# Twelve split pairs, VectorE's layer-1 lows from hi copies in PSUM, and layer 2's split tiles behind the plain tiles of the next slot

## What is computed

```python
for idx, (W, b) in enumerate([(w0, b0), (w1, b1), (w2, b2)]):
    z = relu(einsum('bhd,bkd,hks->bsd', x0, xk, W) + b)
    # layers 0 and 1: first 64 rows are the next xk, the other 64 go to direct;
    # layer 2: all 128 rows go to direct
logit = sum over d of concatenate(direct)           # 256 values a row
h = relu([logit, dense] @ W_top1 + b_top1)          # 272 -> 512
h = relu(h @ W_top2 + b_top2)                       # 512 -> 256
y = h @ W_top3                                      # 256 -> 1
```

## Time and profile before

| | us |
|---|---|
| median of three runs | 2544.88 |
| lowest, highest | 2543.24, 2546.89 |
| the profiled execution, its own time | 2545.02 |
| its span, first to last instruction | 2543.1 |
| TensorE busy | 2432.8 |
| VectorE busy | 2268.7 |
| GpSimd busy | 1557.9 |
| ScalarE busy | 1175.5 |

### The profile page before, as it was taken

How to read it: one execution, slowest core, us unless ns; L and a number is a source line. 1 busy time by engine, 2 the same in 40 slices (tenths; PEclk the granted TensorE clock), 3 DMA queues, 4 the chain that set the end, 5 groups by cost and what they waited for, 6 DMA issues and landing times.

```text
span 2543.1 us, 25999 instructions
## 1 busy us (share of the span) xinstructions
PE 2432.8 (96%) x7712; PEld 1423.5 (56%) x7712; DVE 2268.7 (89%) x1356; ACT 1175.5 (46%) x1414; POOL 1557.9 (61%) x1029
## 2 busy tenths in 40 slices
PE   0599999999999999999999999999999999999999
PEld 0265555556555555555555565555556555555553
DVE  0599999999999999999999999999999999999960
ACT  0244444445454444545444444444444444445442
POOL 6476667667666766766676666667666766743240
PEclk9899999999999999999999999999999999999999
DMA  2986777777677777867777776787777677766610
GB/s 69 246 211 180 199 207 202 180 217 214 176 198 205 207 178 215 209 182 197 209 206 177 217 206 190 190 211 210 178 207 205 200 184 213 207 182 194 195 30 0
DMA packets 262712, 477.02 MB, mean 188 GB/s; under 512 B 19500, under 2 KB 37788, under 8 KB 262614
## 3 DMA queue, kind: packets, MB, share of 16 engines
q1 hardware_dynamic: 141766, 271.07, 38.9%
q10 hardware_dynamic: 100480, 200.29, 28.5%
q0 software_dynamic: 20448, 5.45, 1.4%
HBM read 468.99 MB, written 7.74 MB: 187 GB/s over the span
## 4 chain that ended last, share of the span: by engine, by line
PE 73%; POOL 10%; DVE 6%; issue 4%; DMA 4%; ACT 2%; SPq 0%; POOLq 0%; DVEq 0%; ACTq 0%
PE z L693 37%; PE z L716 33%; POOL emb L352 5%; DVE prod L418 4%; POOL pair_lo L211 4%; DMA emb<-in_tbl,idx 3%; PE xk L775 1%; PE z L775 1%; DMA x_pairs<-x_transposed 1%; ACT pair_hi L532 1%; POOL half_parts L207 1%; DVE pair_lo L211 1%; PE turned L674 1%; DVE logit L448 1%; ACT xk L542 0%
## 5 line engine op out<-in xcount | busy, mean ns | idle before, releaser
L418 DVE TENSOR_TENSOR prod<-x_pairs,xk 128x2048 f32<-128x2048 f32 x640 | 1436.4, 2284 | 75.2 <-PE z L716 46.9
L693 PE MATMUL z<-prod,w_plain 128*128 128x512 f32 (+2 forms) x2944 | 1383.1, 594 | 40.5 <-DVE prod L418 40.5
L532 ACT CAST pair_hi<-prod 128x1024 fp32r<-128x1024 f32 x703 | 735.4, 1046 | 1085.2 <-PE z L716 793.6
L211 POOL TENSOR_TENSOR pair_lo<-prod,pair_hi 128x1024 fp32r<-128x1024 f32 x320 | 764.1, 2388 | 638.3 <-ACT pair_hi L532 621.7
L693 PEld LDWEIGHTS z<-prod,w_plain 128*128 128x128 f32 (+2 forms) x2944 | 555.4, 189 | 474.1 <-issue 394.9
L352 POOL DMA_INDIRECT emb<-in_tbl,idx x624 | 701.3, 1124 | 184.0 <-issue 173.7
L716 PE MATMUL z<-pair_hi,w_lo 128*128 128x512 f32 (+1 forms) x1408 | 786.6, 559 | 2.3 <-DVE pair_lo L211 1.7
L716 PE MATMUL z<-pair_hi,w_hi 128*128 128x512 f32 (+1 forms) x1408 | 555.7, 395 | 0.0
L716 PE MATMUL z<-pair_lo,w_hi 128*128 128x512 f32 (+1 forms) x1408 | 555.1, 394 | 0.0
L211 DVE TENSOR_TENSOR pair_lo<-prod,pair_hi 128x1024 fp32r<-128x1024 f32 (+1 forms) x384 | 468.5, 1220 | 48.7 <-ACT pair_hi L532 48.7
L716 PEld LDWEIGHTS z<-pair_hi,w_lo 128*128 128x128 f32 (+1 forms) x1408 | 265.2, 188 | 297.2 <-POOL pair_lo L211 135.8
(11 more groups left out here) (50 smaller groups left out, 566.5 us busy)
## 6 DMA issues: line engine op xcount, KB each, us to landing
x_pairs<-x_transposed SPq DMA_DIRECT2D x64, 2432.0 KB, 16.9
x_pairs<-x_transposed ACTq DMA_DIRECT2D x64, 2432.0 KB, 19.3
x_diag<-x_transposed SPq DMA_DIRECT2D x128, 546.0 KB
x_diag<-x_transposed ACTq DMA_DIRECT2D x64, 546.0 KB
x_pairs<-x_transposed SPq DMA_DIRECT2D x64, 256.0 KB, 20.4
emb<-in_tbl,idx POOLq DMA_INDIRECT x624, 6.3
x_diag<-x_transposed SPq DMA_DIRECT2D x128, 78.0 KB
x_transposed<-stage SPq DMA_DIRECT2D x32, 156.0 KB
```

The lines of the kernel that those rows point to most:

```text
L211: engine.tensor_tensor(pair_lo[0:rows, pair % PAIR_RING], held[0:rows, at:at + 2, :], pair_hi[0:rows, pair % PAIR_RING].bitcast(F32), ALU. ...
L418: nc.vector.tensor_tensor(prod[0:rows, pos % RING, 0:n, :], a, xk.unsqueeze(1).broadcast_to([rows, n, N]), ALU.mult).then_inc(prod_ready, 1)
L532: nc.scalar.copy(pair_hi[0:rows, pair % PAIR_RING], held[:, at:at + 2, :]).then_inc(hi_ready, 1)
L693: ins = nc.tensor.matmul(z[n][:], w, held[0:rows, i, :], start=(k == 0 and i == plain[0]), stop=(k == last_slot and not here and i == plai ...
```

## The change

- **Splits.** Layer 0 splits a second pair (tiles 2 and 3), so there are 12 pairs a chunk. Each split names the engine of its low: layer 1's third pair goes to GpSimd, all others of layers 0 and 1 stay on VectorE.
- **Rings.** The hi and low parts have six tiles (three pairs), with fixed places.
- **Copies in PSUM.** For layer-1 lows of VectorE, ScalarE rounds the products a second time, into `hi_copy` (two PSUM banks, shared with `turned`) or, for the half tile, into the new PSUM bank `direct01`; VectorE subtracts that copy. A second pair copy waits for the low before it. `direct01` is in PSUM, xk0 shares the bank of xk2; so ScalarE waits for layer 0's last product before it writes xk2.
- **Order on VectorE.** A slot's lows always follow the next slot's product; the exception for slot 1 of layer 1 is gone.
- **Order on TensorE.** Layer 2's split tiles follow the plain tiles of the next slot, which frees each slot later. Layer 0 waits for both its slots, does the three last tiles, then the two split pairs, and frees both slots at the end. The transposes move behind layer 0.
- **GpSimd.** Layer 1's low comes first in a chunk, then 9 or 10 gathers, then layer 2's lows. 20 fields of the second group are ahead at the start instead of 30; the indices are loaded after layer 2's lows of chunk 1, the gathers no longer wait for the earlier ones in each chunk, and fields 30 to 38 are gathered in chunk 1.
- **Sums.** logit01 and logit2 hold 512 rows; SP stores a window of 128 rows per group to DRAM, and `load_top` loads the first 1536 rows and the rest back (four more loads).
- **Stage.** `fill_stage` moves behind the hand-on of xk1 and direct_0 in chunk 1, and ScalarE waits for its own copies there.

```diff
-SPLITS = {0: [(0, 0, 2)],
-          1: [(0, 0, 2), (1, 0, 2), (2, 0, 2), (2, 3, 1), (3, 0, 2), (4, 0, 2)],
-          2: [(0, 0, 2), (1, 0, 2), (2, 0, 2), (2, 3, 1), (3, 0, 2), (4, 0, 2)]}
-EARLY = {1: 4, 2: 4}
+SPLITS = {0: [(0, 0, 2, V), (0, 2, 2, V)],
+          1: [(0, 0, 2, V), (1, 0, 2, V), (2, 0, 2, G), (2, 3, 1, V), (3, 0, 2, V), (4, 0, 2, V)],
+          2: [(0, 0, 2, G), (1, 0, 2, G), (2, 0, 2, G), (2, 3, 1, G), (3, 0, 2, G), (4, 0, 2, G)]}
+EARLY = {1: 5, 2: 4}
+BEHIND = {1: False, 2: True}
-GATHERS_AHEAD = 30
-GATHERS_AT = [range(30, F), range(0, 10), range(10, 20), range(20, 30)]
-PAIR_RING = 2
+GATHERS_AHEAD = 20
+GATHERS_AT = [range(20, 30), range(30, F), range(0, 10), range(10, 20)]
+PARTS = 6
...
             def group(bt, fields_at):
...
+                    done = lows_of(1, chunk, 0, split, pos)
+                    if c == 2 and len(fields_at[c]):
+                        start_group(bt + 2, False)
+                    gather(fields_at[c])
...
+                    lows_of(2, chunk, done, split, pos)
+                    if c == 1 and len(fields_at[2]):
+                        pool.wait_ge(gathered, 16 * (bt + 2) * F)
+                        pool.sem_inc(waits_held, 1)
+                        load_indices(bt + 2)
...
             def group(bt, last):
                 for c in range(CHUNKS):
+                    if c == 0:
+                        sp.wait_ge(summed01, bt * CHUNKS + 1)
+                        store_window(0, bt)
+                    if c == 1:
+                        sp.wait_ge(summed2, bt * CHUNKS + 2)
+                        store_window(1, bt)
                     if c == 2 and not last:
                         store_group(bt + 1)
...
+            def products(n, copies, xk, slot, pos, late, split, chunk):
+                first_tile, rows, tiles = (FIRST_TILE, P, TX) if n else (L0_FIRST, R0, T0)
+                for k, first in enumerate(first_tile):
+                    product(slot + k, pos + k, copies[0:rows, first:min(first + QUAD, tiles), :],
+                            xk[0:rows])
+                    split = subtract(late, split)
+                    late = splits_of(n, pos, k, chunk)
+                return late, split
...
+                        act.wait_ge(slot_free, RING + used_by[place + m - 1] + 1)
+                        nc.scalar.copy(hi_parts[0:rows, place:place + m, :], held[:, at:at + m, :]
                                        ).then_inc(hi_ready, 1)
+                    if n and who == V:
+                        copies = [s for s in SPLITS[n][0:i] if s[3] == V]
+                        if m == 1:
+                            nc.scalar.copy(direct01[0:HALF].bitcast(F32R), held[0:HALF, at, :]
+                                           ).then_inc(hi_copied, 1)
+                        else:
+                            if any(s[2] == m for s in copies):
+                                last = max(j for j, s in enumerate(copies) if s[2] == m)
+                                act.wait_ge(lo_ready[V],
+                                            len(SPLITS[0]) + chunk * LOWS_C[V] + last + 1)
+                            nc.scalar.copy(hi_copy[:, 0:m, :].bitcast(F32R), held[:, at:at + m, :]
+                                           ).then_inc(hi_copied, 1)
...
                     if not (last and c == CHUNKS - 1):
+                        round_splits(0, slice(0, None), slot, pos, used_by, chunk)
+                        act.wait_ge(prod_ready, slot + SL0)
                     hand_on(1, xk2, b1_sb, slot)
...
-                    if c == 1 and not last:
-                        fill_stage(bt + 1)
...
                         hand_on(0, xk1, b0_sb, slot)
-                        act.wait_ge(summed01, chunk + 1)
+                        act.wait_ge(summed01, chunk + 2)
                         direct_0()
+                        if c == 1 and not last:
+                            fill_stage(bt + 1)
+                            act.wait_ge(stage_ready, 2 * (bt + 2))
...
+                    for i in plain:
+                        plain_part(n, t, i, held, k == 0 and i == plain[0], False)
+                    if not BEHIND[n]:
+                        split_parts(n, k, lows)
+                    elif k > 0:
+                        split_parts(n, k - 1, lows)
+                if BEHIND[n]:
+                    split_parts(n, last_slot, lows)
+            def layer0(slot, pos, lows):
+                pe.wait_ge(prod_ready, slot + SL0)
+                held = prod[:, (pos + SL0 - 1) % RING]
+                t = L0_FIRST[SL0 - 1]
+                for i in range(T0 - t):
+                    plain_part(0, t, i, held, i == 0, False)
...
+                for i, (s, place) in enumerate(zip(SPLITS[0], PLACES[0])):
+                    ins = split_part(0, 0, s, place, lows, False, i == len(SPLITS[0]) - 1)
+                    lows[s[3]] = lows[s[3]] + 1
+                ins.then_inc(slot_free, SL0)
```

More of the change, by code:

```diff
@@ L78 @@
 NB = 512
-assert CB < NB < B and len(SPLITS[0]) == 1
+assert CB < NB < B and all(k == 0 for k, _, _, _ in SPLITS[0])
 def top_order():
@@ L357, in group @@
             def group(bt, fields_at):
[L358 to L359 removed]
                 for c in range(CHUNKS):
                     chunk = bt * CHUNKS + c
[L363 to L365 removed]
+                    split, pos = len(SPLITS[0]) + chunk * SPLITS_C, SL0 + c * SLC
@@ new lines, in splits_of @@
+            def splits_of(n, pos, slot, chunk):
+                copies, here = lows(1, V) if n == 2 else 0, []
+                for s, place in zip(SPLITS[n], PLACES[n]):
+                    copy = chunk * COPIES_C + copies if n else None
+                    copies += s[3] == V
+                    if s[0] == slot:
+                        here.append((n, pos, copy, place, *s))
+                return here
+            def products(n, copies, xk, slot, pos, late, split, chunk):
[6 more added lines that the diff above has]
+                return late, split
@@ L456, in sum2 @@
                                         z[2][:].rearrange("p (d b) -> p b d", b=CB),
                                         AXIS.X, ALU.add).then_inc(summed2, 1)
-            def layer(n, copies, xk, slot, pos):
-                return [(n, k, copies, xk, slot + k, pos + k) for k in range(SLX if n else SL0)]
-            products(layer(0, x0_diag, xk0, 0, 0), 0, 0, 0)
+            dve.wait_ge(xk0_ready, 1)
+            late, split = products(0, x0_diag, xk0, 0, 0, [], 0, 0)
+            subtract(late, split)
@@ L490, in group @@
                         if k == 1:
-                            sum01(chunk)
-                    pair = pair_after + PAIRS[2]
+                            sum01(bt, c)
+                        split = subtract(late, split)
+                        late = splits_of(2, pos, k, chunk)
+                    subtract(late, split)
             with dve.Fori(0, GROUPS - 1) as bt:
@@ L677, in transpose_group, with plain_part @@
                         ins.then_inc(turned_ready, 1)
-            def layer(n, slot, pos, split, pair):
-                whole, hi, lo, splits = w_plain[n], w_hi[n], w_lo[n], SPLITS[n]
-                first_tile = FIRST_TILE if n else L0_FIRST
-                last_slot = len(first_tile) - 1
-                for k, t in enumerate(first_tile):
+            def plain_part(n, t, i, held, first, last):
+                rows = P if n else R0_LAST if t + i == T0 - 1 else R0
+                w = w_plain[n][0:rows, PLAIN_TILES[n].index(t + i), :]
+                return nc.tensor.matmul(z[n][:], w, held[0:rows, i, :], start=first, stop=last)
```

310 lines of the change are left out of this document (167 added, 143 removed).

## The result

The changed kernel takes 2575.95 us (four runs, 2574.12 to 2577.07) against 2544.27 before: a ratio of 1.0122, 95% interval [1.0105, 1.014]. The forecast was 2500. The profiled execution took 2574.12 us, 29 more than the one of before.

What follows compares the result with a forecast made beforehand. TensorE's work plus three late layer-2 lows was taken to bound the loop. Ordinary periods -40, transposing ones -4.7 and start +0.6 total -44 us: 2545.0 becomes 2501, 2500 at the median; range 2484 to 2534.

Steps and rivals of the forecast that it cites:

- Ordinary periods: Main-loop chunks without transposes: from 36.69 to 35.8 us, -0.85 x 47 = -40 us.
- The +0.10: Per chunk, us added for what is late next: layer 2's last pair and VectorE's stalled layer-1 product.
- the change does not free layer 2: Rival: layer 2's last pair's low stays late by some 0.5 us a chunk; +25 us, 2525; chance 0.12.
- Prices of VectorE: Layer-1 lows with a PSUM operand stay at 1.22 us; the reduce over direct01 falls from 1.06 to 0.69.
- The slower rival: Layer 1's four pairs: dearer PSUM lows make VectorE the bound; 2600 us, far bound 2780; chance 0.08.
- PSUM copies: Layer 1: lows reading one PSUM operand no longer stretch gathers, which took 1.58 us instead of 0.94.
- Gathers and transposes: Chunk 1: last gather starts near T + 16, transposes wanted at T + 20.6; transposing period 37.5 us.
- gathers late: Rival, before the transposes: gathers land 2 us later than taken, 6.6 us each; +30 us, 2530; chance 0.12.
- the 0.7 taken: Us of wait before the transposes, between no wait with 3.5 us to land and 2.0 with 6.6.
- x_diag: Loads behind SP's stage stores: out at +18, needed by +30; cost zero, margin 2 to 3 us.
- the rival's 2 us: Rival: x_diag loads late once a group, from SP's queue order; 2 us x 15, 2530; chance 0.05.
- Start: Kernel start: xk0's copy goes in front of the first pairs' load, +0.6 us.

Runs made afterwards that it cites:

- e5_stage_early: Changed kernel with three of nine gathers before layer 1's low and the stage copy behind layer 2's first two hi parts; 2500.45 us, ratio 0.9808.
- f3_stage_three: e5_stage_early with the stage copy behind three hi parts of layer 2 instead of two; 2519.57 us, ratio 0.9905.
- e7_sbuf_lows: Changed kernel without ScalarE's PSUM copies, VectorE's layer-1 lows reading the hi parts in SBUF; one run, 2663.44 us.
- e1_early3: Changed kernel with three of chunk 1's nine gathers issued before GpSimd's layer-1 low; 2631.23 us, ratio 1.0329.
- e2_fill3: Changed kernel with three extra plain matmuls, result unused, in front of the transposes; 2553.24 us, ratio 1.0023.
- e3_early1: Changed kernel with one of chunk 1's nine gathers issued before GpSimd's layer-1 low; 2654.71 us, ratio 1.0412.

## Why the prediction was wrong, point by point

- **Ordinary periods: right.** 35.8 us was forecast and measured, and the 41 us they give match the forecast's 40. The weight loads' wait for GpSimd fell from 135.8 us to 3.1. The +0.10 was right by luck. It stood for a late last pair and late products, and neither is there: the end of a chunk with the last pair takes 4.53 us on average in the changed kernel, 4.52 being its undisturbed length. TensorE's own slots, from start to start, add up to 35.8, where the prediction's rounded ones gave 35.7 (its step of 0.85 for 36.69 - 35.8 = 0.89 is another slip of that size). The late last pair came in e5_stage_early, where no stall hands GpSimd any slack: there it costs 0.2 us a chunk on average. The rival "the change does not free layer 2" had this mechanism, at 0.4. The marks of the periods are VectorE's, so a single period can be shorter than TensorE's need (35.38 in f3_stage_three, behind a stall).
- **Prices of VectorE: right.** 1.21 for the PSUM low, -0.375 for the reduce; VectorE works 34.7 us in the ordinary period (34.9 forecast), ScalarE 22.8 (23.6), GpSimd 26.95 (27.0). The slower rival, through dearer PSUM lows, is out, and with it the figures of the Trainium skill (VectorE: DVE Perf Modes, The TRN2 errata), by which a PSUM source has the larger fixed cost. These rows show 1212 against 1213 ns and contradict it for these two forms of 1024 columns.
- **PSUM copies: mis-sized.** The prediction counted stretched gathers only. e7_sbuf_lows puts the copies at 1.7 us a period (one run). It changed no number of the forecast, since the kernel keeps the copies.
- **Gathers and transposes: the step that failed.** The text took the last gather at T + 16, a stretch of 0.8 us, and 3.5 us to land, although the trace of before showed 6.6 for today's last gather. It explained those 6.6 by the pair loads beside it. (In that group TensorE went on 5.96 us after the gather's start, on the same count; but in 11 of 15 groups of that trace TensorE waited for the gathers, up to 0.96 us, and they landed after 6.1 to 6.9 us.) The runs show T + 17.0, a stretch of 1.9 and 6.9 us, with no DMA busy at the end. The rival "gathers late" had the place and the mechanism, and its 2 us over the 0.7 taken come to 2.7, near the 3.2 measured. It was given 0.12 and should have been the forecast: the row with 6.6 was there, and the reason against it was an assumption about the pair loads.
- **The term that was missing: the clock.** The rival's 2530 left out what a stall of TensorE does behind it. It is 2.7 us a group, 40 us in all, nearly as much as the wait itself (3.2 x 15 = 48). Forecast 2500, plus 2.5 x 15 for the wait over the 0.7 taken, plus 40, is 2578, against 2576. No row of before showed TensorE standing still for microseconds in the loop. But the start of that trace had the price: TensorE stands still for 15.5 us before 100.40, the granted clock is 0.50 from 88 us on, and it is back at 1.00 only at 105 us or so, over 4 us after work has resumed.
- **x_diag: cost right here, margin wrong.** No wait in the changed kernel. The margin of 2 to 3 us was the gather stall itself: it holds back layer 1's first product and with it ScalarE's pair load, so that x_diag is ahead by 3.75 us (1223.14 against 1226.89 in the timeline of the result). With the stall gone it is negative, and the rival's 2 us are 10. In e1_early3 the loads go out 17.7 us after the chunk's sum, the copy wants them at 28.0 (forecast 18 and 30), and they land at 38: the term that was mis-sized is the landing beside the pair loads, 20 us where the stated margin leaves 9 to 10. Had the gathers been on time, the time would have been 2631 and not 2500.
- **Start: +0.6 forecast, none measured** (the first sum at 120.51 against 120.57).
- The forecast's number came up in e5_stage_early, by another sum and so by luck: 62 periods of 36.28 instead of 47 of 35.8 and 15 of 37.5.

## What to carry to other kernels

When work of another engine is moved to stand right behind a transfer, price the transfer by the slowest landing in the trace, and price a stall of TensorE with the half-clock stretch behind it, here 2.7 us for a stall of 3.2. Before removing a wait, list what is issued relative to it on every DMA queue: a stall can be what keeps two loads in the right order, and its removal then needs a second edit. Try such edits together as well as one by one.

## What the runs showed of the hardware

- An indirect gather of GpSimd lands 6.7 to 7.2 us after it starts (15 groups of the changed kernel; 6.1 to 6.9 in 11 groups of the kernel before, 6.4 to 7.2 in e2_fill3), in 1212 to 1213 with the DMA engines idle. The time is not fixed from the start: in e3_early1 a last gather that takes 2.82 us itself has landed 6.5 to 6.7 us after its start.
- TensorE idle for 3.2 us: granted clock 0.64 and then 0.50, back to 1.00 some 5.6 us after work resumed. Idle for 0.46 us: 1.00 throughout.
- A gather that starts under two VectorE lows on SBUF operands takes 2.83 us: it ends at 1206.24, 0.82 us after the lows (1205.42). Under lows that read one operand from PSUM gathers take 0.94 to 0.96. The Trainium skill (SBUF — State Buffer, Who interferes with whom) says that a VectorE instruction with two SBUF inputs contends with a GpSimd instruction that reads SBUF, and one with at most one SBUF input does not. For the lows these rows agree, if the gather instruction, which takes its indices from SBUF, counts as such a reader.
- 226 GB/s at a DMA share of 1.06, while x_diag and x_pairs loads overlap (e1_early3), against 204 GB/s at 0.79 in an ordinary period of the changed kernel.
